# Loading the first step's keys beside the setup and staging the feed-forward weights in their own tiles

## The reference

```python
x_act = tanh(x);  static_out = x_act @ W.T
# 16 heads of width 16; q = k = heads(x_act), v = heads(static_out)
lam = sigmoid(lam_logit);  beta = eta * (1 - lam) / 16
S = lam * S;  u = beta * (v_t - S.T @ k_t);  S += k_t u.T;  o_t = S.T @ q_t
y = layernorm(static_out + o) * gamma + ln_beta
x = layernorm(x + y)
h = silu(x @ wg.T) * (x @ wu.T)        # wg, wu: 768 x 256, int32 * 1/127
x = layernorm(x + h @ wd.T)            # wd: 256 x 768, int32 * 1/127
```

## Time and profile before

| | us |
|---|---|
| median of 3 runs | 1876.73 |
| lowest and highest | 1870.12, 1882.23 |
| the profiled execution | 1866.64 |
| its span, first to last instruction | 1864.9 |
| PE, DVE, ACT, POOL busy | 1401.9, 1424.7, 1100.3, 782.9 |

### The profile page before, as it was taken

One profiled execution on the slowest core, in us unless ns is written; L12 is line 12 of the kernel. 1 busy time (PEld: TensorE's weight loads), 2 busy tenths in 40 slices (PEclk: granted clock), 3 DMA queues, 4 the chain that ended last, 5 costly groups with the idle time before them and its releaser, 6 DMA issues.

```text
span 1864.9 us, 53894 instructions
## 1 busy us (share of the span) xinstructions
PE 1401.9 (75%) x21032; PEld 1080.7 (58%) x21032; DVE 1424.7 (76%) x3479; ACT 1100.3 (59%) x2339; POOL 782.9 (42%) x1106
## 2 busy tenths in 40 slices
PE   1344877788888878888888777788877888888764
PEld 0244656566666656666666566666655666666542
DVE  8257878788888878887888887788778887788741
ACT  0223666567666666666666666666666666666544
POOL 6012444344444444454444444444344444454442
PEclk9855887789888878888888788888887888888877
DMA  2445544445555455545644554454455544544200
GB/s 71 87 92 111 99 107 113 106 110 114 112 108 114 113 108 118 105 113 107 113 107 111 109 114 104 107 113 101 110 108 118 105 115 113 110 106 110 68 26 23
DMA packets 704383, 191.01 MB, mean 102 GB/s; under 512 B 624000, under 2 KB 691584, under 8 KB 704128
## 3 DMA queue, kind: packets, MB, share of 16 engines
q1 hardware_dynamic: 704128, 187.57, 47.3%
HBM read 103.55 MB, written 67.11 MB: 92 GB/s over the span
## 4 chain that ended last, share of the span: by engine, by line
SPq 39%; DMA 18%; PE 16%; DVE 10%; issue 8%; ACT 7%; POOL 1%; ACTq 0%; POOLq 0%; DVEq 0%
SPq L977 11%; DMA scr_t<-t 7%; SPq L986 6%; SPq L962 5%; PE pc L175 5%; SPq L947 4%; SPq L938 4%; DMA y_out<-v 4%; DMA xa<-L_attn_x 3%; PE pf L232 3%; SPq L920 3%; SPq L992 2%; DMA scr_x<-xt 2%; PE pd L272 2%; PE pg L240 2%
## 5 line engine op out<-in xcount | busy, mean ns | idle before, releaser
L879 POOL TENSOR_TENSOR hlo<-gate,hhi 128x512 f16<-128x512 f32 x192 | 228.9, 1195 | 325.1 <-ACT hhi L710 324.9
L175 PE MATMUL pc<-R,tb 128*128 128x32 f16 x4096 | 158.1, 189 | 161.7 <-DVE R L362 141.7
L175 PEld LDWEIGHTS pc<-R,tb 128*128 128x128 f16 x4096 | 147.1, 118 | 181.7 <-DVE R L362 156.5
L175 PE MATMUL pc<-S,e 128*128 128x32 f16 x4096 | 157.6, 188 | 61.8 <-DVE S L383 61.7
L175 PEld LDWEIGHTS pc<-U,kb 128*128 128x128 f16 x4096 | 152.0, 118 | 81.4 <-DVE U L370 79.1
L175 PEld LDWEIGHTS pc<-S,e 128*128 128x128 f16 x4096 | 153.1, 118 | 77.4 <-DVE S L383 67.6
L175 PE MATMUL pc<-U,kb 128*128 128x32 f16 x4096 | 159.4, 190 | 49.7 <-DVE U L370 49.6
L209 PEld LDWEIGHTS pf<-xb,e 128*128 128x128 f16 x4096 | 152.8, 118 | 60.1 <-DMA e<-scr_x 42.1
L272 PE MATMUL pd<-wd_t,hhi 128*128 128x256 f16 x768 | 176.7, 276 | 13.7 <-DVE xr L481 8.2
L209 PE MATMUL pf<-xb,e 128*128 128x32 f16 x4096 | 156.3, 191 | 37.4 <-DMA e<-scr_x 36.1
L272 PE MATMUL pd<-wd_t,hlo 128*128 128x256 f16 x768 | 176.3, 276 | 0.0
(11 more groups left out here) (118 smaller groups left out, 3297.4 us busy)
## 6 DMA issues: line engine op xcount, KB each, us to landing
xa<-L_attn_x SPq DMA_DIRECT2D x128, 128.0 KB
scr_x<-xt SPq DMA_DIRECT2D x64, 256.0 KB, 2.1
xb<-scr_x SPq DMA_DIRECT2D x256, 64.0 KB, 2.8
e<-scr_x SPq DMA_DIRECT2D x256, 64.0 KB, 3.6
scr_g<-gs SPq DMA_DIRECT2D x32, 512.0 KB, 2.9
gh<-scr_g SPq DMA_DIRECT2D x256, 64.0 KB, 2.2
kb<-k SPq DMA_DIRECT2D x512, 32.0 KB, 2.3
scr_t<-t SPq DMA_DIRECT2D x64, 256.0 KB
```

The costliest lines, as they stand in the source:

```text
L175: last = pe.matmul(pc2[:, :, cols], stationary(h, a), moving[:, :, cols], start=a == 0, stop=a == 1)
L879: pool.tensor_tensor(hlo[:, t, :], gate[:, t % 2, :], hhi[:, t, :], ALU.subtract).then_inc(SEM["hl"], 1)
```

## The change

The setup is rearranged; nothing in the loop changes but a few waits of SP, each met once or twice.

- The key work of step 0 (load, tanh, transposes, split, store, spread) is taken out of rounds -2 and -1 and put into the setup blocks. SP loads x first of all. Round -2 is gone (FIRST = -1), and round -1 no longer stores and spreads keys.
- The one load semaphore becomes four: constants, W, feed-forward weights, gamma and ln_beta.
- The natural weights are staged in hhi, hlo, res, xr and x1hi instead of E[1] and v. They are cast in place from int32 to fp32 (four casts) instead of to fp16 in tb, and transposed as fp32.
- ACT, not DVE, copies the 18 pairs out of PSUM.
- POOL clears S and E[0], waits for the four casts, and then clears E[1], both halves of kb, and tb.
- DVE makes lam, beta and the powers first, then splits the keys, casts, writes w_t, and goes on with the reversed powers, dcol, kcol and nmask. The fp16 ident is gone.
- SP waits for the cleared tiles at the first use of each, and for the staging to be over before the first residual load.

```diff
-        FIRST, LAST = -2, NS + 3
+        FIRST, LAST = -1, NS + 3
         def sp_spread_keys(sp, q, p):
+            if q == 1:
+                sp.wait_ge(s_pool0, 11)
+                sp.sem_inc(s_hop, 1)
...
         def sp_load_inverse(sp, q, p, g):
+            if q == 0:
+                sp.wait_ge(s_pool0, 14)
+                sp.sem_inc(s_hop, 1)
...
         def sp_load_kb(sp, q, p, g):
+            if q == 0:
+                sp.wait_ge(s_pool0, 14)
+                sp.sem_inc(s_hop, 1)
...
         def sp_load_residual(sp, q, p):
+            if q == 0:
+                sp.wait_ge(s_ps, NJ)
+                sp.sem_inc(s_hop, 1)
         def sp_step(sp, s, p):
-            if live(s + 1):
+            if live(s + 1) and s >= 0:
                 sp_store_keys(sp, s + 1, 1 - p, 0)
...
+        wg_nat, wu_nat = as_nat(hhi[:, :, :]), as_nat(hlo[:, :, :])
+        wd_nat = [a[:, 0:3, :].rearrange("p n d -> p (n d)").bitcast(I32) for a in (res, xr)]
+        ps = [pg[0][:, 0:256], pg[1][:, 0:256]]
         @block.sync
+            sp_load_x(eng, 0, 0)
+            eng.dma_start(sc[:, ETA:ETA + 1], eta.to_broadcast([P, 1])).then_inc(s_ldc, 16)
...
-            eng.wait_ge(s_wt, NJ + 1)
-            eng.wait_ge(s_pool0, 14)
+            eng.wait_ge(s_pool0, 10)
+            sp_store_keys(eng, 0, 0, 0)
+            sp_store_keys(eng, 0, 0, 1)
+            sp_spread_packed_keys(eng, 0, 0)
+            sp_spread_keys(eng, 0, 0)
         @block.gpsimd
+            eng.memset(S[:, :], 0.0).then_inc(s_pool0, 1)
             eng.memset(as_u32(E[0][:, :].rearrange("p z h b i n -> p (z h b i n)")), 0).then_inc(s_pool0, 1)
+            eng.wait_ge(s_cast, 4)
+            eng.memset(as_u32(E[1][:, :].rearrange("p z h b i n -> p (z h b i n)")), 0).then_inc(s_pool0, 1)
             eng.memset(as_u32(kb[:, 0].rearrange("p h b k z m -> p (h b k z m)")), 0).then_inc(s_pool0, 1)
             eng.memset(as_u32(kb[:, 1].rearrange("p h b k z m -> p (h b k z m)")), 0).then_inc(s_pool0, 1)
-            eng.wait_ge(s_wt, NJ + 1)
             eng.memset(as_u32(tb[:, :].rearrange("p g h b i z m -> p (g h b i z m)")), 0).then_inc(s_pool0, 1)
         @block.scalar
-            eng.wait_ge(s_ld, 16 * 8)
+            eng.wait_ge(s_ldc, 32)
             eng.activation(sc[:, OML:OML + 1], sc[:, LOGIT:LOGIT + 1], ACT.Sigmoid, scale=-1.0).then_inc(s_a0, 1)
+            act_activate(eng, 0, 0)
+            act_transpose_keys(eng, 0, 0, 0)
+            act_transpose_keys(eng, 0, 0, 1)
+            for j, (_, dst) in enumerate(jobs):
+                eng.wait_ge(s_ps, j + 1)
+                eng.activation(dst, ps[j % 2], ACT.Copy).then_inc(s_wt, 1)
             eng.wait_ge(s_c, N_SETUP)
         @block.vector
...
+            dve_transpose_keys(eng, 0, 0, 0)
+            dve_transpose_keys(eng, 0, 0, 1)
+            eng.wait_ge(s_ldn, 64)
+            for nat, w32 in ((wg_nat, wg32), (wu_nat, wu32), (wd_nat[0], wd32[0]), (wd_nat[1], wd32[1])):
+                eng.tensor_copy(w32, nat).then_inc(s_cast, 1)
+            eng.wait_ge(s_wps, 1)
             link(eng.tensor_scalar(w_t[:, :, 0, :], w_ps, WS, None, ALU.mult))
...
         @block.tensor
+            pe_transpose_keys(eng, 0, 0, 0)
+            pe_transpose_keys(eng, 0, 0, 1)
+            eng.wait_ge(s_ldw, 16)
...
+            eng.wait_ge(s_cast, 4)
+            for j, (srcs, _) in enumerate(jobs):
+                if j >= 2:
+                    eng.wait_ge(s_wt, j - 1)
+                for a, w32 in enumerate(srcs):
+                    last = eng.transpose(ps[j % 2][:, a * P:(a + 1) * P], w32, ident[:, :])
+                last.then_inc(s_ps, 1)
```

More of the change, by code:

```diff
@@ L143, in build @@
         SEM = {name: sem("s_" + name) for name in PER}
-        s_ld = sem("s_ld")
+        s_ldc = sem("s_ldc")
+        s_ldw = sem("s_ldw")
+        s_ldn = sem("s_ldn")
+        s_ldb = sem("s_ldb")
+        s_cast = sem("s_cast")
+        s_wps = sem("s_wps")
+        s_w = sem("s_w")
         s_hop = sem("s_hop")
@@ L1032, in build @@
         as_u32 = lambda a: a.bitcast(mybir.dt.uint32)
-        ident16 = gate[:, 0, 0:P // 2].bitcast(F16)
         rpowers = gate[:, 1, 0:C]
@@ L1037, in build @@
         block = ctx.enter_context(nc.Block())
[L1039 to L1052, removed]
+        w_nat = x1hi[:, :, :].rearrange("p a n -> p (a n)").bitcast(F32).rearrange("p (a d) -> p a d", a=2)
+        as_nat = lambda a: a.rearrange("p t n -> p (t n)").bitcast(I32).rearrange("p (t d) -> p t d", d=D)
+        wg_nat, wu_nat = as_nat(hhi[:, :, :]), as_nat(hlo[:, :, :])
+        wd_nat = [a[:, 0:3, :].rearrange("p n d -> p (n d)").bitcast(I32) for a in (res, xr)]
+        wg32, wu32 = wg_nat.bitcast(F32), wu_nat.bitcast(F32)
+        wd32 = [a.bitcast(F32) for a in wd_nat]
+        ps = [pg[0][:, 0:256], pg[1][:, 0:256]]
         jobs = []
-        for dst, src in ((wg_t, wg16), (wu_t, wu16)):
+        for dst, src in ((wg_t, wg32), (wu_t, wu32)):
             for half in range(2):
@@ L1060, in build @@
         for t in range(NHT):
-            jobs.append(([wd16[:, a, t * P:(t + 1) * P] for a in range(2)], wd_t[:, t, :]))
+            jobs.append(([wd32[a][:, t * P:(t + 1) * P] for a in range(2)], wd_t[:, t, :]))
         NJ = len(jobs)
-        N_SETUP = 4 + 1 + 8 + 2 * C + 7 + 1 + (C - 1)
+        N_SETUP = 1 + 8 + 2 * C + 7 + 1 + (C - 1)
         @block.sync
@@ L1067, in _ @@
             bc = lambda a, n: a.rearrange("(o n) -> o n", o=1).to_broadcast([P, n])
[L1068 to L1075, removed]
-            eng.wait_ge(s_wt, NJ + 1)
-            eng.wait_ge(s_pool0, 14)
+            sp_load_x(eng, 0, 0)
+            eng.dma_start(sc[:, ETA:ETA + 1], eta.to_broadcast([P, 1])).then_inc(s_ldc, 16)
+            eng.dma_start(sc[:, LOGIT:LOGIT + 1], lam_logit.to_broadcast([P, 1])).then_inc(s_ldc, 16)
+            eng.dma_start(w_nat, W.rearrange("(a p) d -> p a d", p=P)).then_inc(s_ldw, 16)
+            eng.dma_start(wg_nat, w_gate.rearrange("(t p) d -> p t d", p=P)).then_inc(s_ldn, 16)
+            eng.dma_start(wu_nat, w_up.rearrange("(t p) d -> p t d", p=P)).then_inc(s_ldn, 16)
+            for a in range(2):
+                eng.dma_start(wd_nat[a], w_down[a * P:(a + 1) * P, :]).then_inc(s_ldn, 16)
+            eng.dma_start(gamma[:, :], bc(ln_gamma, D)).then_inc(s_ldb, 16)
+            eng.dma_start(lnb[:, :], bc(ln_beta, D)).then_inc(s_ldb, 16)
+            eng.wait_ge(s_pool0, 10)
[3 more added lines that the diff above has]
+            sp_spread_keys(eng, 0, 0)
             all_steps(eng, sp_step)
@@ L1092, in _ @@
             eng.memset(minus[:, :], -1.0).then_inc(s_pool0, 1)
+            eng.memset(S[:, :], 0.0).then_inc(s_pool0, 1)
             eng.memset(as_u32(E[0][:, :].rearrange("p z h b i n -> p (z h b i n)")), 0).then_inc(s_pool0, 1)
+            eng.wait_ge(s_cast, 4)
+            eng.memset(as_u32(E[1][:, :].rearrange("p z h b i n -> p (z h b i n)")), 0).then_inc(s_pool0, 1)
             eng.memset(as_u32(kb[:, 0].rearrange("p h b k z m -> p (h b k z m)")), 0).then_inc(s_pool0, 1)
             eng.memset(as_u32(kb[:, 1].rearrange("p h b k z m -> p (h b k z m)")), 0).then_inc(s_pool0, 1)
-            eng.memset(S[:, :], 0.0).then_inc(s_pool0, 1)
-            eng.wait_ge(s_wt, NJ + 1)
-            eng.memset(as_u32(E[1][:, :].rearrange("p z h b i n -> p (z h b i n)")), 0).then_inc(s_pool0, 1)
             eng.memset(as_u32(tb[:, :].rearrange("p g h b i z m -> p (g h b i z m)")), 0).then_inc(s_pool0, 1)
@@ L1101, in _ @@
             eng.wait_ge(s_c, N_SETUP)
+            eng.wait_ge(s_ldb, 32)
             all_steps(eng, pool_step)
@@ L1121, in _ @@
             eng.wait_ge(s_pool0, 2)
[L1122 to L1134, removed]
             eng.wait_ge(s_a0, 1)
@@ L1146, in _ @@
                                        ALU.mult))
+            dve_transpose_keys(eng, 0, 0, 0)
[4 more added lines that the diff above has]
+            eng.wait_ge(s_wps, 1)
+            w_ps = pu[0][:, :].rearrange("p (a d) -> p a d", a=2)
+            link(eng.tensor_scalar(w_t[:, :, 0, :], w_ps, WS, None, ALU.mult))
+            eng.scalar_tensor_tensor(w_t[:, :, 1, :], w_ps, WS, w_t[:, :, 0, :], ALU.mult, ALU.subtract)\
+               .then_inc(s_w, 1)
             for m in range(C):
@@ L1178, in _ @@
                                          w_nat[:, a, half * P:(half + 1) * P], ident[:, :])
-            last.then_inc(s_ps, 1)
-            eng.wait_ge(s_wt, NJ + 1)
+            last.then_inc(s_wps, 1)
+            eng.wait_ge(s_cast, 4)
[5 more added lines that the diff above has]
+                last.then_inc(s_ps, 1)
+            eng.wait_ge(s_wt, NJ)
+            eng.wait_ge(s_w, 1)
             all_steps(eng, pe_step)
```

## The result

The changed kernel took 1856.90 us in the median of 4 runs (1847.60 to 1858.89); the kernel before took 1877.32 beside it. The ratio is 0.9885, with a 95% interval of 0.9838 to 0.9931: faster by 20.4 us in the median, between 13.0 and 30.4 by the interval. The forecast was 1852, a gain of 24.8. The profiled execution took 1857.69 us, its span is 1855.9, only 9.0 less than that of the earlier trace rows.

The account below looks back on a forecast made before the run. The serial setup (staging, clearing, keys) was taken to delay the first Gram; overlapped, it leaves PSUM at 43.4 instead of 68.3, behind held nmask. Gain 24.8 us takes the median from 1876.7 to 1851.9; range 1838 to 1860.

Parts of the forecast that it names:

- Its path: Setup: nmask on DVE, held under POOL's clearing, ends at 42.6 and sets the first Gram's exit from PSUM at 43.4.
- the first rival: nmask not held: setup ends at 28.5, first Gram taken out at 30.9, gain 37.4 us, median 1839.3; chance 0.12.
- Loads: Setup loads with x first: tanh from about 7.7, w_down landed at 14.5 to 15.1, casts starting at 14.9.
- Casts: Four in-place casts to fp32 on DVE: 0.96 and 0.55 us each, 3.1 with gaps, done at 18.0.
- Clearing: POOL clears E[1], both halves of kb and tb after the casts: 20.7 us, from 18.1 to 38.8.
- w_t: DVE writes w_t behind the casts in 1.4 us, not held by the memsets, done at 19.5.
- the second rival: w_t or another earlier DVE instruction is held too: gain 19.0 us, median 1857.7; with slow casts, chance 0.08.
- nmask: DVE's 15 diagonals: first held until clearing ends at 38.8, the other 14 take 3.75 us, setup ends at 42.6.
- Staging: PE's fp32 transposes and ACT's copies of 18 pairs end at some 29.5, hidden behind DVE; cost 0.
- Keys: Early keys: split done at 14.8, Gram matmuls possible 14.4 us later at 29.2, hidden by 13 us.
- The sum: First Gram out of PSUM at 43.4 instead of 68.3: gain 24.8 us, span 1840.1, median 1851.9.
- the third rival: Steady pace changes: intervals 0.8 us longer eat the gain, 1.4 us make it 1% slower; chance 0.10.

Follow-up runs that it names:

- e2: The changed kernel with nmask's 15 diagonals written by a tensor-by-tensor product instead of a product with a scalar; median 1840.78 us, ratio 0.9824 to the kernel before.
- e1: The changed kernel unaltered, run again for a second trace; median 1855.61 us, ratio 0.9903 to the kernel before.
- e7: The kernel before, unaltered, a single execution for a second trace; mean interval between Gram stores 53.34 us.
- e8: The changed kernel with the 18 pairs copied out of PSUM by DVE, behind w_t, instead of ACT; ratio 0.9859 to the kernel before, gain 24.6 us.
- e12: The changed kernel with the 18 copies on DVE instead of ACT, run once more; ratio 0.9849 to the kernel before, gain 30.0 us.
- e5: The changed kernel with the key work of step 0 put back into rounds -2 and -1; ratio 0.9973 to the kernel before, gain 3.7 us.
- e4: The changed kernel with a second memset of tb on POOL ahead of the last one; ratio 0.9919 to the kernel before, gain 12.6 us.
- e6: The changed kernel with POOL clearing both halves of kb ahead of its wait for the casts; ratio 0.9849 to the kernel before, gain 26.6 us.
- e3: The changed kernel with tensor-by-tensor diagonals and DVE splitting the keys before the powers of lam; ratio 0.9809 to the kernel before, gain 33.5 us.

## Why the prediction was right

The prediction's mechanism held, and its sum missed one term, the pace.

*Its path.* It had put the start at the end of nmask, held under POOL's clearing, and not at the keys or the staging. The trace shows that: ACT waited 14.20 us for nmask, up to 43.22, while the keys' matmuls had begun at 30.67. It came from one row, the 3329 ns of the earlier trace rows that ended with a memset of the earlier trace rows; e2 shows the cause by taking the form away, and its start (31.46) is close to the 30.9 that the first rival gave for a free nmask.

*Loads.* Tanh began at 8.51, not 7.7, and the casts at 16.37, not 14.9. The load of lam_logit took 4.2 us from issue to landing behind x, where the earlier trace rows had 3.3; and w_down's two DMAs took 1.45 and 1.62 us to issue, not 0.6. This was the largest miss among the terms of the start, 1.5 us.

*Casts.* 0.96 and 0.55 us, as taken; done at 19.1 instead of 18.0.

*Clearing.* From 19.19 to 39.95: 20.8 us, with 20.7 forecast.

*w_t.* Its second half ran at 19.77 for 0.69 us under a memset, and both parts were over at 20.5: the second rival is out.

*nmask.* Three long diagonals and twelve short ones, end at 43.18 against 42.6. The casts were 1.1 late; the two diagonals that passed early gave 0.5 of it back, which the sum had not counted on. The sentence that DVE doesn't get in between two memsets was wrong as a rule: here it did, twice, and in e1 three times. What hangs on it is small but more than the 0.3 us given for it: three diagonals that pass early are three times 0.27, 0.8 us.

*Staging.* Done at 28.6 on PE and 29.0 on ACT, 29.5 forecast, and covered by 14 us. *Keys:* matmuls at 30.67 against 29.2, covered too.

*The sum.* Gram 0.6 late, stored at 49.28 against 48.6. The start's gain was 24.4 for 24.8. The measured median lies 5.0 us over the forecast: 0.4 is the start, 0.6 the median before, which is 1877.32 with its fourth run, and 4.0 were lost after the start. For this last part the sum had nothing, and the number came out near because the part was small. It belongs to the third rival, steady pace, which had a chance of 0.10 at a larger size. Its sign had been named too: a mean interval off 53.07 by over 0.3 us, and the trace has 53.54. By that sign the prediction was wrong in one point, though the kernel before itself came close to it with 53.34 in e7. The reason "no order inside the loop is touched" was true and settled nothing. By e8 and e12 the engine of the copies is the likely cause, some 0.13 us an interval (4.0 / 31); a scatter of the first batch alone would leave the other seven losses unexplained.

## What to carry to other kernels

Before clearing tiles on GpSimd beside VectorE work, look in the trace for VectorE instructions whose end coincides with a memset's: a short one that took 3.3 us once can cost 14 where more clearing lies over it, and a two-tensor form of the same product (172 ns) runs through. Put clearing that nothing holds back under the loads and not behind them: moving two memsets was worth 6.7 us of start. A gain in the setup mostly carries to the end (here 24.4 us of start gave 18 to 20), and to size it within a few us take medians of batches: the 13 runs of the kernel before beside e1 reach from 1866.3 to 1886.0.

## What the runs showed of the hardware that was not expected

Whether a waiting VectorE instruction gets in between two back-to-back memsets varies: the cast of the earlier trace rows missed three boundaries; the first diagonal missed one of them in the kernel after and in e5, three in e4 (14.56 us), and none in e1 and e6 (0.78 us). The kernel after and e1 are one program, so the code alone doesn't decide it. The rows do not tell why.

A small DMA issued behind 2.6 MB of weight loads came late: the keys' store in e3 was followed by its spread after 6.1 us instead of 2.3. And with the loads of x ahead of it, the first load of w_down took 1.2 to 1.8 us to issue in each of nine traces, and the second 0.5 to 1.9, against 0.61 and 0.56 in e5, which has the same two loads without x ahead. In the kernel after, gamma and ln_beta right behind them took 0.43 each.

With 18 copies of the setup moved from DVE's list to ACT's, PE's wait for a DMA in the steady loop was about 16 us instead of about 11, in all but one of the traces; that the copies cause it is likely and not proven, and the way stays open.
